# Attention probabilities scaled on GpSimd before the transpose, values stationary in four partition groups

## The reference, cut to what matters

```python
x = rmsnorm(hidden, ln1_w)
q, k, v = ((x @ W.T).reshape(b, s, 16, 16) for W in (Wq, Wk, Wv))       # 16 heads of 16
scores = einsum('bqhd,bkhd->bhqk', q, k) / 4
probs  = softmax(where(causal, scores, min), axis=-1)
attn   = einsum('bhqk,bkhd->bqhd', probs, v).reshape(b, s, 256) @ Wo.T
mod    = 0.1 * tanh(attn @ A)                                           # A: 256 x 16
h      = rmsnorm(hidden, ln2_w)
gate   = silu(h @ W_in.T + mod * (h @ A) @ B);  up = h @ W_up.T
out    = hidden + (gate * up) @ W_down.T
```

## Time and profile before

| | |
|---|---|
| median of three runs | 1255.88 us |
| lowest, highest | 1253.8, 1260.31 us |
| span of the profiled execution, first to last instruction | 1202.4 us |
| its own device time | not given; the median is 53.5 us above the span |
| busy share of the span | PE 89%, PE weight loads 76%, DVE 55%, ACT 28%, POOL 31% |
| mean granted PE clock | 0.952 of 2.4 GHz |

### The profile page before, as it was taken

The page is one execution under the profiler, slowest core; times in us unless marked ns, Lnnn a source line. Parts: engine busy times, 40 slices in busy tenths (PEclk is TensorE's granted clock), DMA queues, the critical chain, the costliest instruction groups (busy, mean ns, idle before and its releaser), DMA issues.

```text
span 1202.4 us, 23243 instructions
## 1 busy us (share of the span) xinstructions
PE 1073.1 (89%) x6341; PEld 916.0 (76%) x6341; DVE 664.0 (55%) x2185; ACT 340.2 (28%) x858; POOL 375.2 (31%) x522
## 2 busy tenths in 40 slices
PE   4468999999999999999999899549999999999966
PEld 4356788888888788888888787329888888888855
DVE  1733445665765765665666555354555555555546
ACT  1023334333333243243243341001111111111243
POOL 0410011141141150150240320434555555555521
PEclk8777899999999999999999999779999999999989
DMA  9249960050240320410410500139999999999776
GB/s 356 69 97 295 287 126 1 10 150 10 54 115 0 87 80 0 105 63 0 111 48 0 127 33 1 54 100 282 297 314 305 302 307 305 306 289 302 250 275 229
DMA packets 129984, 184.56 MB, mean 153 GB/s; under 512 B 29749, under 2 KB 100117, under 8 KB 127517
## 3 DMA queue, kind: packets, MB, share of 16 engines
q1 hardware_dynamic: 94720, 104.41, 32.2%
q10 hardware_dynamic: 22989, 45.89, 11.1%
q0 software_dynamic: 12240, 33.83, 7.8%
HBM read 122.99 MB, written 61.60 MB: 154 GB/s over the span
## 4 chain that ended last, share of the span: by engine, by line
PE 58%; issue 16%; DVE 9%; DMA 7%; POOL 4%; ACT 3%; ACTq 1%; SPq 0%; DVEq 0%; POOLq 0%
PE bank L891 10%; PE bank L900 9%; PE bank L597 6%; PE bank L584 4%; PE bank L764 4%; PE bank L592 4%; PE bank L766 4%; DMA w_in<-in_e_w 3%; PE bank L725 3%; PE bank L641 2%; PE bank L652 2%; PE bank L722 2%; PE bank L826 2%; POOL x_rows L552 2%; PE bank L845 1%
## 5 line engine op out<-in xcount | busy, mean ns | idle before, releaser
L565 POOL DMA_INDIRECT y_rows<-sh_gu,ids x133 | 131.3, 987 | 59.9 <-POOL spare L283 56.7
L981 ACT ACTIVATE prob<-bank,nmx 128x128 f32<-128x128 f32 (+1 forms) x256 | 90.4, 420 | 176.0 <-DVE nmx L1252 175.6
L1047 ACT ACTIVATE inv<-bank 88x256 f32<-88x256 f32 x159 | 60.5, 380 | 273.3 <-PE bank L891 267.8
L1252 DVE TENSOR_REDUCE nmx<-bank 128x2 f32<-128x512 f32 (+1 forms) x96 | 66.1, 689 | 98.2 <-PE bank L700 95.8
L900 PE MATMUL bank<-w_in,inv 88*128 88x256 f32 x428 | 109.8, 379 | 0.0
L1480 DVE COPY sh_gu<-bank 128x256 f32<-128x256 f32 x133 | 56.5, 425 | 95.6 <-PE bank L900 95.5
L552 POOL DMA_INDIRECT x_rows<-x_row,desti x96 | 96.3, 1003 | 28.5 <-issue 28.5
L900 PEld LDWEIGHTS bank<-w_in,inv 88*128 88x128 f32 x428 | 72.7, 190 | 6.0
L597 PE MATMUL bank<-cst,prob 128*128 128x128 f32 x384 | 59.8, 279 | 10.2 <-ACT probT L987 10.2
L764 PE MATMUL bank<-h2T,w_up 128*128 128x256 f32 x256 | 66.5, 382 | 0.0
L766 PE MATMUL bank<-h2T,w_in 128*128 128x256 f32 x256 | 65.7, 379 | 0.0
(11 more groups left out here) (260 smaller groups left out, 2204.0 us busy)
## 6 DMA issues: line engine op xcount, KB each, us to landing
w_in<-in_e_w ACTq DMA_DIRECT2D x107, 176.0 KB
w_down<-in_e_w SPq DMA_DIRECT2D x105, 176.0 KB
x_rows<-zeros SPq DMA_DIRECT2D x2, 8192.0 KB, 36.8
fwd<-x_rows SPq DMA_DIRECT2D x78, 132.0 KB, 4.7
w_up<-in_e_w SPq DMA_DIRECT2D x54, 176.0 KB
w_up<-in_e_w ACTq DMA_DIRECT2D x52, 176.0 KB
w_down<-x_rows SPq DMA_DIRECT2D x54, 132.0 KB
stack_q<-q_parts SPq DMA_DIRECT2D x16, 384.0 KB, 5.8
```

The costliest lines, as they stand in the source:

```text
L565: pool.indirect_dma_start(y_rows, bass.IndirectOffsetOnAxis(ap=ids[s][:].bitcast(U32), axis=0), yc[s], None).then_inc(S[f"m_st{s}"], 16)
L981: i = act.activation(prob[:, u % 2, h * w:(h + 1) * w], psum(u % 2, h * w, (h + 1) * w), ACT.Exp, bias=nmx[:, u, h:h + 1])
L1047: act.activation(hs[n], bank[0:IH, 3 + n, 0:2 * P].rearrange("p (a b) -> p a b", a=2), ACT.Silu).then_inc(S["m_hs"], 1)
L1252: dve.tensor_reduce(nmx[:, u, 0:512 // w], bank[:, u % 2, :].rearrange("p (h k) -> p h k", k=w), AX, ALU.max, negate=True).then_inc(S["b_m ...
```

## The change

- The probabilities are normalised before they are transposed. ACT's exp also gives the row sums (`accum_out`), DVE takes their reciprocal one slot later (`b_rec`), and POOL multiplies prob by it in place (`b_scaled`, new part on POOL: slot u+1 runs `unit(u)`). `turn_probs` waits for `b_scaled` and moves one slot back, to slot u+2, `values` to u+3. prob has three buffers instead of two, probT four.
- In `values` the operands change sides: the values of a head are stationary (128x32, the upper 16 columns zero), probT moves (128 columns), and the four heads of a group of matmuls write to four groups of 32 partitions of bank 3, accumulating over the head groups. For the last 128 queries two units are handled together, in every second slot.
- Wv, Wo and A are folded per head once, in turn 0 (`b_wvo`), so that a head's product is already its part of `attn @ A`. What is left at the end is the copy of bank 3 (`mixed`) and one matmul with a 0/1 matrix (`gather`) that adds the partition groups. `divide`, the transposes of att and attT go.
- The mask matmul writes only the 128 columns of each head that hold the diagonal: 4 x 128 for units 0 to 3 as before, 2 x 128 for units 4 to 11.
- Some tiles share memory to make room (att with d_k, mh with mixed, pos with ex, hit with sact, zeros with sgt; the first copy into sgt waits for the fills of x_rows), and cst is 256 columns wider.

```diff
-        masks = [csb[:, 640 - w:640].rearrange("p (o k) -> p o k", o=1).broadcast_to([P, 4 * P // w, w]) for w in (P, L)]
+        masks = [csb[:, 384:512].rearrange("p (o k) -> p o k", o=1).broadcast_to([P, n, P]) for n in (4, 2)]
...
-        v1 = sb("v1", [P, TT, HEADS, HD + 1])
-        UNITS = GROUPS + 2 * GROUPS
-        nmx = sb("nmx", [P, UNITS, 4])
-        prob, probT = sb("prob", [P, 2, 512]), sb("probT", [P, 2, 4, P])
-        rec = sb("rec", [P, TT, HEADS])
-        attT = sb("attT", [P, KT, L])
-        woa = sb("woa", [P, KT, P])
-        th, mh = sb("th", [P, L]), sb("mh", [P, L])
+        v1 = sb("v1", [P, TT, HEADS, PAIR])
+        UNITS, PVS = GROUPS + 2 * GROUPS, 2 * GROUPS
+        PROBS, PROBTS = 3, 4
+        nmx, sums, rec = (sb(n, [P, UNITS, 4]) for n in ("nmx", "sums", "rec"))
+        prob, probT = sb("prob", [P, PROBS, 512]), sb("probT", [P, PROBTS, 4, P])
+        mixed = sb("mixed", [P, L])
+        b_wvo = sb("b_wvo", [P, KT, D])
+        th, mh = sb("th", [P, L]), mixed
...
-        TURN = """A1 A1b D1 A1q u0 D2k A1k u1 D2x A2 u2 D2v A3a u3 A3b u4 A3p D2q D2w u5 t0 D3 u6 D3n A4a u7 D3o D4 A4b A4z
-            u8 S0 u9 A5 u10 A5n D4l S1 u11 A5o D4m S2 A6n u12 SDa u13 t1 A6o D4t SDb SD B6a B6c B6b C1 f0 D4k f1 C2 f2 D5 f3 D5p C2v
+        TURN = """A1 A1b D1 A1q u0 D2k A1k u1 D2x A2 u2 D2v A3a u3 A3b u4 A3p D2q D2w u5 D3 u6 D3n A4a u7 D3o D4 A4b A4z
+            u8 S0 u9 A5 u10 A5n D4l S1 u11 A5o D4m S2 A6n u12 SDa u13 A6o D4t SDb SD u14 B6a B6c B6b C1 f0 D4k f1 C2 f2 D5 f3 D5p C2v
...
-            pool.memset(v1[:, :, :, HD:HD + 1], 1.0)
+            pool.memset(v1[:, :, :, HD:PAIR], 0.0)
...
+            def unit(u):
+                w = P if u < GROUPS else L
+                n = 512 // w
+                def part(b):
+                    pool.wait_ge(S["b_rec"], b * UNITS + u + 1)
+                    p = prob[:, u % PROBS, :].rearrange("p (h k) -> p h k", k=w)
+                    r = rec[:, u, 0:n].rearrange("p (h o) -> p h o", o=1).broadcast_to([P, n, w])
+                    pool.tensor_tensor(p, p, r, ALU.mult).then_inc(S["b_scaled"], 1)
+                return part
...
+                         "B8": inverse_root("B"), **{f"u{u + 1}": unit(u) for u in range(UNITS)}})
...
+                    if dh == 1 and first(b):
+                        pe.wait_ge(S["ld_b"], 96)
+                        for eh in range(KT):
+                            for kt in range(KT):
+                                mm = pe.matmul(psum(1, eh * P, (eh + 1) * P), b_wo[:, kt, eh * P:(eh + 1) * P],
+                                               b_a[:, kt, :], start=(kt == 0), stop=(kt == KT - 1))
+                        mm.then_inc(S["set_woa"], 1)
...
+                    pe.wait_ge(S["set_heads"], 1)
+                    for dh in range(KT):
+                        for et in range(KT):
+                            mm = pe.matmul(psum(1, dh * D + et * P, dh * D + (et + 1) * P), b_w["v"][:, et, dh * P:(dh + 1) * P],
+                                           woa[:, et, :], start=True, stop=True)
+                    mm.then_inc(S["set_wvo"], 1)
...
-                by_token(psum(4), h1T, b_w["v"]).then_inc(S["b_v"], 1)
+                if first(b):
+                    pe.wait_ge(S["set_wvo_out"], 1)
+                by_token(psum(4), h1T, b_wvo).then_inc(S["b_v"], 1)
...
-                pe.matmul(bank[:, n, :].rearrange("p (h k) -> p h k", k=w), identb, masks[u >= GROUPS], start=True, stop=False,
-                          skip_group_check=True)
+                pe.matmul(bank[:, n, :].rearrange("p (h k) -> p h k", k=w)[:, :, w - P:w], identb, masks[u >= GROUPS],
+                          start=True, stop=False, skip_group_check=True)
...
-                pe.wait_ge(S["b_exp"], b * UNITS + u + 1)
+                pe.wait_ge(S["b_scaled"], b * UNITS + u + 1)
                 if u:
                     need(pe, "b_pT_out", b * UNITS + u)
                 for j in range(4):
-                    t = turn(psum(2, j * P, (j + 1) * P), prob[:, u % 2, j * P:(j + 1) * P])
+                    t = turn(psum(2, j * P, (j + 1) * P), prob[:, u % PROBS, j * P:(j + 1) * P])
...
-                if u == GROUPS:
-                    pe.wait_ge(S["b_att"], b * 2 + 1)
-                for h, (g, eh, par) in enumerate(unit_heads(u)):
-                    head = eh * 8 + 2 * g + par
-                    out = psum(3, head * (HD + 1), (head + 1) * (HD + 1))
-                    if u < GROUPS:
-                        mm = pe.matmul(out, probT[:, u % 2, h, :], v1[:, 0, head, :], start=True, stop=True)
-                    else:
-                        for kt in range(TT):
-                            mm = pe.matmul(out, probT[:, u % 2, 2 * h + kt, :], v1[:, kt, head, :],
-                                           start=(kt == 0), stop=(kt == TT - 1))
+                if u < GROUPS:
+                    for j, (g, eh, par) in enumerate(unit_heads(u)):
+                        mm = pe.matmul(bank[j * PAIR:(j + 1) * PAIR, 3, 0:P], v1[:, 0, eh * 8 + 2 * g + par, :],
+                                       probT[:, u % PROBTS, j, :], start=(g == 0), stop=(g == GROUPS - 1))
+                else:
+                    both = [(v, h, *at) for v in (u - 1, u) for h, at in enumerate(unit_heads(v))]
+                    for kt in range(TT):
+                        for j, (v, h, g, eh, par) in enumerate(both):
+                            mm = pe.matmul(bank[j * PAIR:(j + 1) * PAIR, 3, P:L], v1[:, kt, eh * 8 + 2 * g + par, :],
+                                           probT[:, v % PROBTS, 2 * h + kt, :], start=(g == 0 and kt == 0),
+                                           stop=(g == GROUPS - 1 and kt == TT - 1))
                 mm.then_inc(S["b_pv"], 1)
 
             def unit(u):
                 def part(b):
                     if u < UNITS:
                         scores(b, u)
-                    if 1 <= u <= UNITS:
-                        turn_probs(b, u - 1)
-                    if 2 <= u:
-                        values(b, u - 2)
+                    if 2 <= u < UNITS + 2:
+                        turn_probs(b, u - 2)
+                    if 3 <= u < GROUPS + 3 or u > GROUPS + 3 and u % 2 == 0:
+                        values(b, u - 3)
...
-            def B6a(b):
-                pe.wait_ge(S["b_att"], b * 2 + 2)
-                turn_tiles(psum(0), att).then_inc(S["b_attT"], 1)
...
-                pe.wait_ge(S["b_attT_out"], b + 1)
-                for kt in range(KT):
-                    mm = pe.matmul(psum(1, 0, L), woa[:, kt, :], attT[:, kt, :], start=(kt == 0), stop=(kt == KT - 1))
-                mm.then_inc(S["b_mod"], 1)
+                pe.wait_ge(S["b_mixed"], b + 1)
+                pe.matmul(psum(1, 0, L), gather, mixed[:], start=True, stop=True).then_inc(S["b_mod"], 1)
...
-                        need(act, "b_pT", b * UNITS + u - 1)
+                        need(act, "b_pT", b * UNITS + u - PROBS + 1)
                         w = P if u < GROUPS else L
                         for h in range(512 // w):
-                            i = act.activation(prob[:, u % 2, h * w:(h + 1) * w], psum(u % 2, h * w, (h + 1) * w), ACT.Exp,
-                                               bias=nmx[:, u, h:h + 1])
+                            i = act.activation(prob[:, u % PROBS, h * w:(h + 1) * w], psum(u % 2, h * w, (h + 1) * w), ACT.Exp,
+                                               bias=nmx[:, u, h:h + 1], accum_out=sums[:, u, h:h + 1])
                         i.then_inc(S["b_exp"], 1)
-                    if 1 <= u <= UNITS:
-                        need(act, "b_pT", b * UNITS + u)
-                        need(act, "b_pv", b * UNITS + u - 2)
-                        act.activation(probT[:, (u - 1) % 2, :, :], bank[:, 2, :].rearrange("p (j q) -> p j q", j=4), ACT.Copy
+                    if 2 <= u < UNITS + 2:
+                        need(act, "b_pT", b * UNITS + u - 1)
+                        need(act, "b_pv", b * PVS + pvs_of(u - 2 - PROBTS))
+                        act.activation(probT[:, (u - 2) % PROBTS, :, :], bank[:, 2, :].rearrange("p (j q) -> p j q", j=4), ACT.Copy
...
-                act.wait_ge(S["b_attT"], b + 1)
-                need(act, "b_mod", b)
-                act.activation(attT[:], psum3(0), ACT.Copy).then_inc(S["b_attT_out"], 1)
+                act.wait_ge(S["b_pv"], (b + 1) * PVS)
+                need(act, "b_mh", b)
+                act.activation(mixed[:], psum(3, 0, L), ACT.Copy).then_inc(S["b_mixed"], 1)
...
+                    dve.tensor_tensor(woa, psum(1, 0, KT * P).rearrange("p (k r) -> p k r", k=KT),
+                                      same_head.rearrange("p (o r) -> p o r", o=1).broadcast_to([P, KT, P]), ALU.mult
+                                      ).then_inc(S["set_heads"], 1)
...
+                    if u:
+                        n = 4 if u - 1 < GROUPS else 2
+                        dve.wait_ge(S["b_exp"], b * UNITS + u)
```

(54 more changed lines are left out.)

70 lines of the change are left out of this document (39 added, 31 removed).

## The result

The changed kernel takes 1264.82 us (median of 20 runs, 1262.01 to 1272.27), the kernel before 1255.73 us beside it: ratio 1.0075, 95% interval 1.0056 to 1.0093. It is slower by 9 us, where 42 were forecast; 1264.8 lies inside the range of 1258 to 1332 by that range's width, not by the sum. The profile ahead of the prediction (span 1202.4) is as on N, the times beside it as on S. In every later run the time is about 2 us above the span.

What follows compares the result with a forecast made beforehand. PE's instruction stream was taken to set the 85.5 us turn. Five turns of +7.5 (+37.5), turn 8 +10, turn 2 -3.3 and turn 1 -2 gave +42 on 1255.88: 1298 us, range 1258 to 1332.

Steps and rivals of the forecast that it cites:

- The hold-up: Turns 3 to 7: PE's turn_probs(0) waits for scale(0), behind the previous turn's twelve indirect DMAs (D6) on POOL: 8.05 us each.
- The clock: PE's granted clock halves behind the 8 us gap: +2.3 us per turn (0 if not, 4.6 if twice as long).
- POOL not held, the other side: Rival: scale(0) runs between two indirect DMAs, so hold-up and clock cost go; -25 us, 1231; chance 0.06.
- The saved work: PE work saved per turn with attention, from values, mask and the turn's end: 7.1 us.
- Values: PE's values matmuls, 12 units a turn: 0.35 us each instead of 0.80, saving 5.4 us per turn.
- serial groups: Rival: the four partition groups don't overlap, a unit of values costs 0.87 us; +28 us, 1326; chance 0.18.
- Secondary waits: PE waits for late hand-overs from DVE, POOL and ACT: sum 5.0, net 3.8 us per turn (ends 0 and 6).
- x_row: PE's wait before x_row's transposes, behind DVE's work after scores(7): 1.25 us, one of the secondary waits.
- exp's sum on ACT: Cost of exp also summing rows on ACT: 0 to 0.33 us per unit, taken as 0.
- the +10: Turn 8, without A parts: turn_probs(0) 10.75 us late, with clock, savings and secondary waits +10 us in all.
- the last one of the sum: From span to time: 1202.4 becomes 1244.6, and 53.5 us between span and median is kept, giving 1298.
- The light rival: Rival: values at 0.22 us a unit and no secondary waits; total -2 us, 1254, no change; chance 0.10.

Runs made afterwards that it cites:

- N: Kind of chip on which the kernel before takes 1204 to 1207 us; the changed kernel takes 1264 us there.
- S: Kind of chip on which the kernel before takes 1248 to 1256 us, with stalls; the changed kernel takes 1264 us there.
- e4: e3 with two swaps in the order of parts (A4b ahead of D4, u12 ahead of A6n): 1196.6 to 1198.3 us on both kinds of chip.
- e5: The kernel before, with six of D6's twelve indirect DMAs moved ahead of C2h and B8: 1206.3 us on S (before 1253.2).
- e8: The kernel before, with three of the twelve indirect DMAs ahead of C2h and B8 and nine behind: 1200.2 us, twice, on N (before 1206.6).
- e3: The changed kernel, with six of D6's twelve indirect DMAs moved ahead of C2h and B8: 1215.5 us on S (before 1248.5).
- e7: e4 with the scaling of all units on DVE, none on POOL: 1189.5 us on N (before 1206.6).
- e1: The changed kernel, with units 0 to 2 scaled on DVE instead of POOL: 1208.6 us on N, 1257.5 us on S.

## Why the prediction was right and wrong

**The hold-up, right.** 8.05 forecast and 0.44 for the transposes of unit 0, which move behind it and leave PE waiting earlier: 8.49 together, where the gap measures 8.46 (N) and 8.14 (S), released by scale(0) behind the twelfth DMA. The clock: +2.3 forecast; on S transposes 1.12 instead of 0.63 and eight matmuls 3.62 instead of 1.99 are +2.1, on N it is +2.0. POOL not held, the other side, is out.

**The saved work, nearly right.** Values 0.35 a unit, as forecast, and 0.29 where two units follow one another (0.57 for 16 records): serial groups are out. The page "TensorEngine Tiling (Array Packing)" of the Trainium skill, section "Key Properties", lets tiles run in parallel, and the trace agrees (8 records in 0.35, against 0.87 in the earlier trace rows). PE's busy time falls by 5.9 to 6.5 us a turn, not 7.1. A part is that turn_probs now hands over to values after 0.54 (562.12 to 562.66), before after 0.44, seven times a turn. Another may be that busy time includes the end of the last record ahead of each wait, and there are more waits; how much that is isn't measured.

**Secondary waits, too small.** I had net 3.8. On N PE is idle for 7.7 us a turn besides the hold-up (95.58 - 79.43 - 8.46), before for 2.0 (85.54 - 83.50): net 5.7. x_row was priced at 1.25 and took 1.86; its two operations take 1.44 where the earlier trace rows have 0.73. I took 0 for exp's sum on ACT. It is a separate instruction of 0.20 behind each exp, and moves the next exp from 0.25 to 0.345 behind the last, so four heads take about 0.37 longer, just over the upper end:

```profile
563.13 0.37 ACT L1001 ACTIVATE prob<-bank,nmx 128x128 f32<-128x128 f32 x1 [4.10 <-DVE nmx L1283]
563.39 0.19 ACT L1001 ACTIVATION_READ_ACCUMULATOR prob<-bank,nmx 128x1 f32 x1
563.49 0.36 ACT L1001 ACTIVATE prob<-bank,nmx 128x128 f32<-128x128 f32 x1
```

Together a turn grows by 8.46 + 2.0 - 6.1 + 5.7 = 10.1 (10.0 by the marks), where I had 7.5. Turn 2, without D6 in front, is 84.3 long against 84.0, not 3.3 shorter: there too the saved work became waits (with e4's swaps it is 81.1). Behind the mark of turn 7, turn 8 and all after it, 556.0 - 546.8 = 9.2, near the +10. On N the forecast was thus 42 against 54 in the spans (1259.1 - 1205.2) and 57 in the times. The spans flatter it: the changed kernel's first mark stands 6.0 earlier (141.6 against 147.5), and over all profiles that mark scatters by 8.

**The step that failed** is the last one of the sum: "its difference from the median of the three runs, 53.5, is taken to stay". It isn't time around the span (about 2 us are). Most of it, 1248 to 1256 against 1204 to 1207, lies in the turns that have D6 in front: 3.7 us in turn 3, 7.3 on average in turns 4 to 7, 9.8 in turn 8, lost in the same stretch, from scores(2) to the twelfth indirect DMA, in which I put the new wait. The two don't add. On chips of kind S, as the times are from, the change turns 92.8 us into 95.5 a turn: +2.7 instead of +7.5, and 9 us in all. The light rival's 1254 is nearer to 1264.8 than my 1298, but by luck: it had no secondary waits, and they are there. The median and the span of one kernel were a view that I had read and not explained; a rival "the 53 us are stalls in the turns" belonged in the range's lower part.

## What to carry to other kernels

Before adding a span's difference to a median, explain the gap between them: if the profile isn't of a run like those timed, a new wait may fall where time is already lost. Split long runs of indirect DMAs in POOL's order and put nothing that PE soon needs behind them; here that was worth 47 us on S (e5) and about 5 on N (e8, another split). Check the first turn as well as the repeating ones: in the changed kernel the same split cost 8 to 9 us once (e3, e4). When PE's work in a full turn is cut, look at each hand-over's slack first: all of the 6 us saved became waits until two pairs of parts changed places.

## What the runs showed of the hardware that was not expected

- On some chips DVE and ACT stood still for up to 9.8 us while POOL issued twelve indirect DMAs in a row, with their inputs ready; on others, with the same kernel, never. Two runs of six don't do it (e3, e4, e5). Which part of the chip stalls isn't shown; shorter remote waits in the expert loop (up to 3.4 us) are seen on the same chips with the split too.
- With six indirect DMAs moved forward in the changed kernel, POOL stood still for 8.4 to 9.4 us ahead of the very first one (e3, e4), and for 0.6 when it had no scaling to do (e7).
- Two DVE operations on 128x256 took 1.44 us with POOL's 128x512 scaling beside them, 0.73 without, on chips of both kinds. The first takes 0.39 as ever; the second, 1.13 instead of 0.41, ends 0.15 after POOL's. With the scaling on DVE (e7) they take 0.73 again. In the changed kernel on N:

```profile
577.23 1.44 DVE L1145 TENSOR_SCALAR x_row<-d_kv,mvD,yD 128x256 f32<-128x256 f32 x2
577.39 1.13 POOL L535 TENSOR_TENSOR prob<-prob,rec 128x512 f32<-128x512 f32 x1 [1.34 <-DVE rec L1289]
```

- PE's granted clock fell to 0.54 once, behind gaps none of which was above 1.86 us (e1); the turn before it, with the same gaps, kept 1.00.
